# A recommendation kernel: fewer sums of gathered rows in the counting passes and more beside the logits, a lane's turns closer together, stores of logits issued by ScalarE

## The reference

```
gathered = item_embeddings[clip(sequence_ids - 1, 0)]        # [2048, 200, 512]
pooled   = where(ids != 0, gathered, 0).sum(1) / max(count, 1)
user     = pooled @ W_rec.T + b_rec                           # [2048, 512]
retrieved = item_embeddings[retrieved_indices].mean(1)        # 50 rows of each user
gate     = sigmoid(concat([user, retrieved]) @ gate_W.T + gate_b)
fused    = gate * user + (1 - gate) * retrieved
logits   = fused @ proj_W.T + proj_b                          # [2048, 12500]
```

## Time and profile before

| | us |
|---|---|
| median of 3 runs (2335.43 to 2343.23) | 2339.99 |
| the profiled execution | 2341.4 |
| its span, first to last instruction | 2339.7 |
| busy: TensorE | 2157.0 |
| busy: VectorE | 1491.0 |
| busy: ScalarE | 717.6 |
| busy: GpSimd | 1123.8 |

### The profile page before, as it was taken

One profiled execution on the slowest core, in us unless ns is written; L12 is line 12 of the kernel. 1 busy time (PEld: TensorE's weight loads), 2 busy tenths in 40 slices (PEclk: granted clock), 3 DMA queues, 4 the chain that ended last, 5 costly groups with the idle time before them and its releaser, 6 DMA issues. The chain is left out here.

```text
span 2339.7 us, 31173 instructions
## 1 busy us (share of the span) xinstructions
PE 2157.0 (92%) x12548; PEld 1099.0 (47%) x12548; DVE 1491.0 (64%) x1701; ACT 717.6 (31%) x947; POOL 1123.8 (48%) x830
## 2 busy tenths in 40 slices
PE   5669999888899888999999898999999999999999
PEld 4545555444545444444444343444444444444444
DVE  8998999676788766334477775876444444443343
ACT  6856775343444333222311111221121100111110
POOL 5673541888858888757368887788000000000000
PEclk7569999999999899999999999999999999999999
DMA  9998995999978999969588898888524445544553
GB/s 303 333 198 273 311 316 202 267 245 236 256 238 263 233 252 280 373 226 344 169 270 297 292 305 255 287 283 295 188 92 159 161 160 172 171 166 157 169 171 115
DMA packets 205198, 554.76 MB, mean 237 GB/s; under 512 B 20992, under 2 KB 104192, under 8 KB 201728
## 3 DMA queue, kind: packets, MB, share of 16 engines
q1 hardware_dynamic: 127424, 334.62, 41.3%
q0 software_dynamic: 77632, 218.16, 34.1%
HBM read 416.21 MB, written 136.48 MB: 236 GB/s over the span
## 5 line engine op out<-in xcount | busy, mean ns | idle before, releaser
L949 PE MATMUL pooled_ps<-mid,ring 128*128 128x512 f16 x3136 | 749.3, 388 | 20.9 <-DVE mid L593 7.9
L449 POOL DMA_INDIRECT gathered<-emb,ret_rows x462 | 565.9, 1225 | 236.8 <-issue 135.3
L755 DVE SCALAR_TENSOR_TENSOR ring<-pooled_ps,out_scale,counts 128x500 f32<-128x500 f32 x320 | 235.3, 736 | 355.4 <-PE pooled_ps L1022 351.0
L949 PEld LDWEIGHTS pooled_ps<-mid,ring 128*128 128x128 f16 x3136 | 298.3, 100 | 346.0 <-issue 54.4
L1022 PE MATMUL pooled_ps<-counts,keys 128*128 128x500 f16 x1920 | 427.5, 380 | 13.9 <-DVE ring L755 11.7
L471 POOL DMA_INDIRECT gathered<-emb,ret_rows x184 | 346.9, 1885 | 145.7 <-DVE keys L570 81.5
L1022 PE MATMUL pooled_ps<-counts,mid 128*128 128x500 f16 x1920 | 411.8, 374 | 0.0
L931 PE MATMUL count_ps<-keys,row_hots 128*128 128x98 f16 x4096 | 289.0, 228 | 108.1 <-DVE keys L570 92.6
L568 DVE TENSOR_TENSOR row_hots<-pair_columns,keys 128x2048 f16<-128x2048 f16 x256 | 312.6, 1221 | 60.3 <-PE count_ps L931 59.4
L931 PEld LDWEIGHTS count_ps<-keys,row_hots 128*128 128x128 f16 x4096 | 257.4, 109 | 191.9 <-DVE keys L570 108.7
L610 DVE TENSOR_TENSOR gathered<-gathered 128x1024 f32<-128x1024 f32 x182 | 223.2, 1226 | 158.0 <-DMA gathered<-emb,ret_rows 145.5
(11 more groups left out here) (96 smaller groups left out, 1036.6 us busy)
## 6 DMA issues: line engine op xcount, KB each, us to landing
logits<-ring SPq DMA_DIRECT2D x100, 1000.0 KB, 5.3
ring<-emb_parts SPq DMA_DIRECT2D x147, 512.0 KB, 5.6
counts<-proj_t SPq DMA_DIRECT2D x50, 1000.0 KB, 8.5
counts<-emb SPq DMA_DIRECT2D x14, 1792.0 KB, 10.5
mid<-emb SPq DMA_DIRECT2D x49, 512.0 KB, 8.1
emb_parts<-ring SPq DMA_DIRECT2D x49, 512.0 KB, 5.9
counts<-proj_b SPq DMA_DIRECT2D x50, 250.0 KB, 5.7
gathered<-emb,ret_rows POOLq DMA_INDIRECT x662, 5.8
```

Of the source, the lines that this page charges most:

```text
L449: pool.indirect_dma_start(slots[group][:, a], None, source, column(block, r * SLOT + a))\
L755: dve.scalar_tensor_tensor(rows[:, r % ROW_SLOTS, v], logit_ps[n % BANKS][:, 0:W], out_scale[:, t % 2, j // 4:j // 4 + 1], bias[:, t % 2], ...
L949: last = pe.matmul(pooled_ps[:, m], ring_v[:, p % RING, c, part, m * P:(m + 1) * P], cvt[:, p % CVT, c], start=(i == 0 and c == 0 and part ...
```

## The change

ADDS_PASS goes from (0, 44, 88, 152) to (0, 34, 68, 140): 34, 34 and 72 additions in passes 1, 2 and 3 in place of 44, 44 and 64, and 148 behind tiles 4 to 151 in place of 136 behind tiles 4 to 139. Lane 2 takes a turn every second batch, at batches 6 to 30 in place of 6 to 42; lane 3 at batches 46 to 70 in place of 58 to 94. The lanes' stores and two loads of retrieved rows move with them. The later dense pieces of group 3 and its mix stand 11 to 13 tiles later, with the guard on the shared sums at strip 24. SyncE no longer issues the stores of logits; ScalarE does, each at the third tile of the next four.

```diff
@@ -41,12 +41,12 @@
 
 PIECES_PASS = {0: (7, 8, 9, 10, 11, 12, 13, 14, 15, 16, 17, 18), 1: (27, 28, 29, 30, 31, 32, 33, 34, 35, 36, 37, 38)}
 PIECES_LOGITS = {2: (58, 60, 62, 64, 66, 67, 68, 69, 71, 73, 75, 77),
-                 3: (102, 104, 106, 108, 150, 151, 152, 153, 155, 157, 159, 161)}
+                 3: (102, 104, 106, 108, 163, 164, 165, 166, 168, 170, 172, 174)}
 
 MIX_PASS, SUM_PASS, LOW_PASS = {0: 20, 1: 40}, {0: 23, 1: 43}, {0: 24, 1: 44}
-MIX_LOGITS, SUM_LOGITS, LOW_LOGITS = {2: 79, 3: 163}, {2: 84, 3: 166}, {2: 86, 3: 168}
-
-ADDS_PASS = (0, 44, 88, 152)
+MIX_LOGITS, SUM_LOGITS, LOW_LOGITS = {2: 79, 3: 176}, {2: 84, 3: 179}, {2: 86, 3: 181}
+
+ADDS_PASS = (0, 34, 68, 140)
 
 
 class Plan:
...
@@ -359,14 +359,6 @@  SyncE
-            def store_rows(r):
...
-                sp.wait_ge(logits_moved, ROWS * (r + 1))
-                sp.dma_start(out.rearrange("(b p) i -> p b i", p=P)[:, first:first + ROWS, c * W:(c + 1) * W],
-                             rows[:, r % ROW_SLOTS]).then_inc(rows_stored[r % ROW_SLOTS], 16)
...
@@ -417,12 +409,8 @@
                     load_strip(t + 2)
                 if t == 11:
                     load_pool(3)
-                store_rows(2 * t)
                 if t + 1 < 2 * NS:
                     load_bias(t + 1)
-                store_rows(2 * t + 1)
-            for s in range(ROW_SLOTS):
-                sp.wait_ge(rows_stored[s], 16 * len(range(s, 4 * NS, ROW_SLOTS)))
 
 
         @block0.gpsimd
@@ -506,19 +494,19 @@
                     store_lane(0)
                     store_lane(1)
                 for turn in range(turns):
-                    if index == 6 + 3 * turn:
+                    if index == 6 + 2 * turn:
                         if turn == 0:
                             wait_ret_stored(pool, 0)
                         gather_lane(2, turn)
-                    if index == 58 + 3 * turn:
+                    if index == 46 + 2 * turn:
                         if turn == 0:
                             wait_ret_stored(pool, 2)
                         gather_lane(3, turn)
-                if index == 56:
+                if index == 44:
                     store_lane(2)
-                if index == 100:
+                if index == 80:
                     store_lane(3)
-                if index == 102:
+                if index == 82:
                     load_ret(0)
                 if index == 126:
                     load_ret(1)
@@ -860,6 +848,14 @@
                     act.wait_ge(logits_made, HALF_BLOCKS * (t - 1))
                 act.activation(strip_parts[:, t % 2, 0], strip[:, t % 2], ACT.Copy, scale=strip_scale[:, c:c + 1])\
                     .then_inc(strip_high, 1)
+
+            def store_rows(r):
+                t, q = divmod(r, HALF_BLOCKS // ROWS)
+                half, c = divmod(t, NS)
+                first = half * HALF_BLOCKS + q * ROWS
+                act.wait_ge(logits_moved, ROWS * (r + 1))
+                act.dma_start(out.rearrange("(b p) i -> p b i", p=P)[:, first:first + ROWS, c * W:(c + 1) * W],
+                             rows[:, r % ROW_SLOTS]).then_inc(rows_stored[r % ROW_SLOTS], 16)
 
             act.wait_ge(columns_made, 1)
             act.activation(norm[:, 0:1], ones_f[:, 0:1], ACT.Sigmoid)
@@ -905,6 +901,11 @@
                 dense_step(n, PIECES_LOGITS, MIX_LOGITS, SUM_LOGITS)
                 if j == 2 and t + 1 < 2 * NS:
                     high_strip(t + 1)
+                if n >= ROWS + 2 and n % ROWS == 2:
+                    store_rows(n // ROWS - 1)
+            store_rows(LAST // ROWS - 1)
+            for s in range(ROW_SLOTS):
+                act.wait_ge(rows_stored[s], 16 * len(range(s, 4 * NS, ROW_SLOTS)))
 
 
         @block0.tensor
@@ -987,7 +988,7 @@
-                wait_sums_read((0, 1, 12, 22)[g], g)
+                wait_sums_read((0, 1, 12, 24)[g], g)
...
-                wait_sums_read(c, 1 if c == 0 else 2 if c < 12 else 3 if c < 22 else 4)
+                wait_sums_read(c, 1 if c == 0 else 2 if c < 12 else 3 if c < 24 else 4)
```

More of the change, by code:

```diff
@@ L360, in load_bias @@
                              .broadcast_to((P, W))).then_inc(bias_in[t % 2], 16)
-            def store_rows(r):
-                t, q = divmod(r, HALF_BLOCKS // ROWS)
-                half, c = divmod(t, NS)
-                first = half * HALF_BLOCKS + q * ROWS
-                sp.wait_ge(logits_moved, ROWS * (r + 1))
-                sp.dma_start(out.rearrange("(b p) i -> p b i", p=P)[:, first:first + ROWS, c * W:(c + 1) * W],
-                             rows[:, r % ROW_SLOTS]).then_inc(rows_stored[r % ROW_SLOTS], 16)
             load_ids(0)
```

## The result

The changed kernel takes 2325.06 us (median of 7 runs, 2320.03 to 2331.27) against 2339.99 (7 runs beside it): ratio 0.9941, interval 0.9922 to 0.996. It is faster, by 15 us where 33 were predicted: inside the stated range of 2288 to 2330 us, outside the 2296 to 2320 that the forecast itself was given. The profiled execution took 2322.34 us, its span is 2320.6.

A forecast was written before the change was run, and what follows sets the result against it. GpSimd's issue of gathers was taken to set the pace until the last addition, then TensorE alone. Span 2339.7 - 30.4 - 2 = 2307.3, forecast 2307 us, within 2296 to 2320 (0.65); wider range 2288 to 2330.

The forecast's parts named there:

- closed sum for pass 1: Pass 1: batch and lane gathers, landing and remaining pairs added up; it ends at 642.5, 17.5 us earlier.
- due pairs for pass 2: Pass 2: lane 3 starts after the fifth addition, at pair 6; the pass takes 238 us against 256.
- work behind the last addition: Logits after 1649: 12 more tiles stand ahead of the gathers' end, 30.4 us less, plus 2 us for the mix.
- 2 us for the mix of the last group: Logits after the additions: the mix moves from tile 163 to 176, where TensorE waits less for squares; 2 us off.
- stores at zero: Stores of logits issued by ScalarE instead of SyncE: zero on both sides, up to 10 us if a dense move is held.
- load of the retrieved rows stays hidden: Last group's dense pieces beside the logits: they shift 11 or 12 tiles, as the last addition does; zero.
- this, not the shorter passes, is the gain: After 1649: the 30.4 us of 12 tiles is the gain; shorter passes only let TensorE get ahead.
- GpSimd's sum of work is the same: Additions beside the logits: only idle time moves GpSimd's end; the last addition is taken as unmoved at 1649.
- rival on the other side: Passes 1 and 2 do not shorten; 13 batches issued later add 41.2 us against 30.4 and 2 won: 2349, chance 0.08.
- ledger: GpSimd's idle time between 390 and 1649 us: 113 us now, 122 after, taken as no move of the last addition.
- bound of 30 us for dearer gathers: Lane gathers beside denser VectorE work, 0.05 x 600 = 30 us later; as a rival 2337, chance 0.05.
- rival of 8 us: Beside the logits: 24 moved gathers cost what they cost with VectorE idle, 8 us less, 2299; chance 0.04.

The follow-up runs named there:

- e3: The changed kernel with the stores of logits given back to SyncE: 2322.31 us, ratio 0.9915 to the kernel before.
- e4: The kernel before with only the stores of logits moved to ScalarE: 2338.86 us, ratio 0.9992.
- e2: The changed kernel with group 2's dense pieces, mix and scaling eight tiles later: 2304.73 us, ratio 0.9843 to the kernel before.
- e8: e2 with twelve additions from beside the logits put into pass 3 (34, 34, 84 and 136): 2306.49 us, ratio 0.9853 to the kernel before.
- e9: e2 with 44 additions each in passes 1 and 2, lane turns every third batch, 148 beside the logits: 2336.32 us, ratio 0.9968 to the kernel before.

## Why the prediction was right and wrong

**Right.** That GpSimd's issue of gathers paces the additions. The closed sum for pass 1 (to 642.5; measured 641.8) and the due pairs for pass 2 (238 us; measured 235). The start of the logits, 1140 against 1137. The work behind the last addition, 32.4 us less against 33.8. The 2 us for the mix of the last group: the timeline of TensorE after, which answers to the earlier trace rows:

```profile
1755.71 0.35 PE L993 MATMUL spare_ps<-fused_sq,ones_f 128*128 128x1 f32 x2 [2.94 <-DVEq L633]
```

The stores at zero, by e3 and e4. The gathers beside the logits at about their old price (387.42/297 = 1.304 us against 1.287).

**Wrong in size: the load of group 2's rows.** The prediction took the dense pieces' shift at zero because "the load of the retrieved rows stays hidden", and said so of the last group alone. Group 2 keeps its tiles and its batch, so it was not looked at, though what lies between the two changed: the logits begin 37 us earlier and the load stays where the gathers are. The rows for it were there: load issued at 1350.2, piece at 1384.5. Move the second by the 37 us that the prediction itself had worked out and it stands at 1347, ahead of the load's issue. The term was set at zero and measured 20 us (2325.06 against e2's 2304.73): the last addition, which was to stay where it was, at 1646.9, comes at 1661.6, and at 1642.9 in e2. None of the rivals had it.

**Wrong in reason, though the sum came out: "this, not the shorter passes, is the gain".** The failing step is "GpSimd's sum of work is the same, so its end moves by its idle time alone", with the tiles then called the whole gain. Idle time depends on where additions stand. With 72 additions in pass 3 GpSimd waits 38 us there for additions; with 84 (e8) 3.3 us, and it ends 28 us earlier, which pays for the 30.4 us of tiles. And with the long passes (e9) the tiles give 5 us, since 12 more additions beside the logits take 26 us there (496.8 against 470.4). An addition moved beside the logits costs 2.2 to 3.5 us of that stage, from the pairs before and e9, and e8 and e2 (504.5 - 462.7 = 41.8 us for 12), and brings one tile of 2.53. The prediction's own rival on the other side said as much, for there the gain is gone when the passes do not shorten.

That the end nearly stood still in e2 is luck in part. The ledger foretold 122 us of idle time for the new kernel, and e2 has 121. But the 113 us of the kernel before are 132: they leave out the 7.3 us above, 2.0 us for slots in mid and most of the waits for landings. So idle time fell by 11 us where it was to rise by 9, and dearer gathers put 15 us on the other side (911 to 926).

**The rival on the other side** assumed 13 x 3.17 = 41.2 us for the moved additions if the passes did not shorten. e9 comes near that case, with the long passes though not with the closer turns: 28.6 us, and the end is 5 us earlier, not 9 later. The price of 41.2 took every moved gather as added time; part of them fills waits, as GpSimd's for slots beside the logits fall from 28.0 to 18.6 us.

**Two small slips.** By its own terms the last addition alone would allow pass 1 to end at 629 us, not 633 (32 batches are 98.9 us). And VectorE's share in pass 1 was not to rise to 80%, since ten additions leave with the 17 us; it stayed at 75% (190.72 of 253).

**The gathers' price.** The bound of 30 us for dearer gathers was half met: GpSimd is busy for 1142.5 us against 1123.8, and a batch gather in passes 1 and 2 costs 1.338 and 1.297 us (99.00/74 and 84.32/65) where the earlier trace rows give 1.245 and 1.212. The share is no guide to this; what stands beside the gathers is. In pass 1 65 of 74 of them now overlap a VectorE instruction with both inputs in SBUF, before 64 of 94, and those that do cost the same (1.39 against 1.38 us). The rival of 8 us overlooked it the other way: beside the logits an addition stands with every tile, so few gathers find VectorE at a move alone. Dearer gathers are not the cause of the miss, since e2 has them too (1150.5 us busy) and is 20 us faster.

## What to carry to other kernels

When a change shifts one engine against another, list every point where an order on the one meets an order on the other, also those whose numbers the diff leaves alone, and write the lead of each (here 34 us) against the shift (here 37). A gain should be ascribed to an edit only after each edit has been tried without the other: here the two halves gave 35.5 and 5.1 us alone and 37.3 together, so a correct sum rested on the wrong half. And an engine's idle time may not be carried over from the profile of before as a constant: ask which additions, placed where, would fill it.

## What the runs showed of the hardware

The issue of a gather, always the same instruction and the same shape, takes 0.94 us at least and up to 2.87 in the changed kernel, and what VectorE does meanwhile decides: 0.95 us when nothing runs there or only instructions with at most one tensor input in SBUF, 1.36 on the mean beside one with both inputs in SBUF, and 2.56 beside a low part of 2.29 us. I had taken it for a price by stage.

Splitting stores and loads over two queues shortened the landing of the 1000 KB loads from 8.6 to 5.6 us and lengthened the stores' from 5.3 to 6.1, at the same DMA traffic; the time did not move, since neither was waited for.
